# Storing transposed tokens once in fp32, with plain fp32 products for the router and the shared expert

## The reference

```python
# layernorm of x, q = x Wq, k and v from a context of 77 rows plus one null row, 16 heads of 64
x = x + jnp.tanh(g_xattn[0]) * _L0_xattn_ref(_layernorm(x, axis=-1), ctx_2048, ...)
x = x + jnp.tanh(g_ffn[0]) * _L0_ffn_ref(_layernorm(x, axis=-1), ...)

# inside _L0_ffn_ref; T = 8192 tokens, H = 256, I = 128, E = 32 experts, K = 8
logits = jnp.dot(x.astype(jnp.float32), Wr) + br
aff = jax.nn.sigmoid(logits)
top_v, top_i = jax.lax.top_k(aff, K)
top_w = top_v / (jnp.sum(top_v, axis=-1, keepdims=True) + 1e-09)
shared = jnp.dot(silu(jnp.dot(x, Wg_s) + bg_s) * (jnp.dot(x, Wu_s) + bu_s), Wd_s) + bd_s
gate = silu(jnp.einsum('th,ehi->eti', x, Wg) + bg[:, None, :])
up = jnp.einsum('th,ehi->eti', x, Wu) + bu[:, None, :]
down = jnp.einsum('eti,eih->eth', gate * up, Wd) + bd[:, None, :]
routed = jnp.einsum('te,eth->th', w_full, down)
return (shared + routed).reshape(b, s, h)
```

## Time and profile before

| | |
|---|---|
| median of 3 runs | 2115.05 us |
| the profiled execution, its own time | 2113.24 us |
| its span, first to last instruction | 2111.5 us |
| PE busy | 1992.3 us, 94% |
| DVE busy | 1669.5 us, 79% |
| ACT busy | 1387.4 us, 66% |
| POOL busy | 1205.2 us, 57% |
| DMA | 625.61 MB, 296 GB/s over the span |
| granted PE clock, mean | 0.982 |

### The profile page before, as it was taken

One profiled execution on the slowest core, in us unless ns is written; L12 is line 12 of the kernel. 1 busy time (PEld: TensorE's weight loads), 2 busy tenths in 40 slices (PEclk: granted clock), 3 DMA queues, 4 the chain that ended last, 5 costly groups with the idle time before them and its releaser, 6 DMA issues.

```text
span 2111.5 us, 42587 instructions
## 1 busy us (share of the span) xinstructions
PE 1992.3 (94%) x13762; PEld 1831.6 (87%) x13762; DVE 1669.5 (79%) x3996; ACT 1387.4 (66%) x4030; POOL 1205.2 (57%) x1323
## 2 busy tenths in 40 slices
PE   7999699999999999999996899999999999999995
PEld 7888589999999999999986789889898888888884
DVE  4333158888888888888887766668999999999996
ACT  4322277777777777777773367777777777777771
POOL 0100104777777777777777400017777777777775
PEclk9999899999999999999998999999999999999997
DMA  9664788877787777777786999999999999999998
GB/s 276 214 191 174 254 241 273 282 241 242 240 246 245 240 240 245 245 245 246 236 268 226 353 323 287 284 295 385 404 404 402 400 393 391 399 394 388 399 359 282
DMA packets 401108, 625.61 MB, mean 296 GB/s; under 512 B 170999, under 2 KB 275160, under 8 KB 398424
## 3 DMA queue, kind: packets, MB, share of 16 engines
q1 hardware_dynamic: 351736, 488.60, 68.5%
q0 software_dynamic: 49152, 134.28, 17.7%
HBM read 315.08 MB, written 307.63 MB: 295 GB/s over the span
## 4 chain that ended last, share of the span: by engine, by line
PE 42%; DVE 19%; DMA 14%; POOL 11%; issue 8%; SPq 3%; ACT 3%; DVEq 0%; POOLq 0%; ACTq 0%
DMA w_raw<-in_experts 13%; POOL pages_dram L929 6%; PE ring L147 4%; PE ring L149 3%; PE ring L148 3%; PE bank L147 3%; PE bank L149 3%; PE bank L148 3%; DVE parts L1881 3%; PE xps L1978 3%; DVE minus_max L1094 2%; PE sim L1355 2%; DVE outT_l L1241 2%; PE gate_ps L147 2%; PE yps L147 2%
## 5 line engine op out<-in xcount | busy, mean ns | idle before, releaser
L1772 POOL DMA_INDIRECT parts<-results_dram,kept_index x512 | 515.7, 1007 | 383.3 <-DMA results_dram<-y 221.9
L929 POOL DMA_INDIRECT pages_dram<-rows,kept_index x512 | 511.1, 998 | 156.0 <-issue 139.1
L1010 ACT ACTIVATE exps<-sim,minus_max 128x78 f32<-128x78 f32 x1024 | 321.7, 366 | 28.1 <-DVE minus_max L1094 27.4
L1010 ACT ACTIVATION_READ_ACCUMULATOR exps<-sim,minus_max 128x1 f32 x1024 | 252.4, 247 | 0.0
L1793 ACT ACTIVATE w_h<-w_raw 128x768 fp32r<-128x768 f32 x159 | 134.1, 843 | 146.9 <-DMA w_raw<-in_experts 146.6
L1881 DVE SCALAR_TENSOR_TENSOR parts<-parts,kept_weight 128x256 f32<-128x256 f32 x448 | 214.1, 478 | 2.1 <-DMA parts<-dense_dram 1.0
L1978 PE MATMUL xps<-ident,xin 128*128 128x128 f32 x1272 | 166.9, 274 | 17.4 <-DVE wq_l L1843 7.4
L1855 DVE TENSOR_TENSOR w_l<-w_raw,w_h 128x768 fp32r<-128x768 f32 x159 | 151.9, 956 | 37.1 <-ACT w_h L1793 36.7
L147 PE MATMUL yps<-w_h,hid_h 128*128 128x256 f32 x636 | 180.6, 284 | 0.1
L148 PE MATMUL yps<-w_h,hid_l 128*128 128x256 f32 x636 | 179.8, 283 | 0.0
L149 PE MATMUL yps<-w_l,hid_h 128*128 128x256 f32 x636 | 179.7, 283 | 0.0
(11 more groups left out here) (261 smaller groups left out, 6576.7 us busy)
## 6 DMA issues: line engine op xcount, KB each, us to landing
xin<-pages_dram SPq DMA_DIRECT2D x159, 512.0 KB, 10.8
results_dram<-y SPq DMA_DIRECT2D x159, 512.0 KB, 9.7
w_raw<-in_experts SPq DMA_DIRECT2D x159, 385.0 KB, 9.5
pages_dram<-blank SPq DMA_DIRECT2D x108, 512.0 KB, 3.3
pages_dram<-blank SPq DMA_DIRECT2D x20, 1024.0 KB, 6.5
values_dram<-values SPq DMA_DIRECT2D x16, 1024.0 KB
v_main<-values_dram SPq DMA_DIRECT2D x64, 256.0 KB
keys_dram<-keys SPq DMA_DIRECT2D x16, 616.0 KB, 4.5
```

The lines of the kernel that those rows point to most:

```text
L929: pool.indirect_dma_start(dram["pages"], bass.IndirectOffsetOnAxis(ap=kept_index[:, at:at + 1].bitcast(U32), axis=0), buffer(batch)[:, k / ...
L1010: last = act.activation(exps[u % 2][:, h, :], scores(u)[:, h // 4, h % 4, :], ACT.Exp, bias=minus_max[u][:, h:h + 1], accum_out=row_sum[u] ...
L1772: pool.indirect_dma_start(parts[slot(batch, t)][:, k, :], None, done, bass.IndirectOffsetOnAxis(ap=kept_index[:, at:at + 1].bitcast(U32), ...
```

## The change

The transposed tokens are one fp32 tile `x2T`, stored to one DRAM tensor. DVE makes no low part of them, and L multiplies `x2T` by the raw router weight in fp32: four matmuls instead of eight, one bias addition instead of two. In the dense rounds `gate_up` multiplies the raw shared weights (`shared_whole`) by the fp32 tokens: four fp32 matmuls instead of twelve fp32r ones, and SP loads one tile of tokens instead of two. Only the shared down weight is still split, so the two splitting instructions on ACT and DVE shrink from 768 to 256 columns. The page rounds stay as they are. Two waits move: SP stores `x2T` once ACT has evicted it, and the wait for the early zero fill goes from ACT to `load_ahead` on SP.

```diff
-    x2T = [sb(f"x2T_{s}", [P, DC, N], F32R) for s in "hl"]
+    x2T = sb("x2T", [P, DC, N])
-    router_w = sb("router_split", [P, DC, 2, ROUTED], F32R)
...
         def load_ahead():
+            sp.wait_ge(stores.filled_ahead, 16 * FLIGHT * AHEAD_FILLS // AHEAD_PAGES)
...
-                sp.wait_ge(ring_lo, nth(EVICTED, "N2", b))
-                for cols, part in zip(x2_cols, x2T):
-                    sp.dma_start(cols[:, :, (b - 2) * N:(b - 1) * N], part[:, :, :].bitcast(F32)).then_inc(x2_stored, 16)
+                sp.wait_ge(ring_hi, nth(EVICTED, "N2", b))
+                sp.dma_start(x2_cols[:, :, (b - 2) * N:(b - 1) * N], x2T[:, :, :]).then_inc(x2_stored, 16)
...
-            act.wait_ge(stores.filled_ahead, 16 * FLIGHT * AHEAD_FILLS // AHEAD_PAGES)
-            act.activation(ahead["shared_split"][0][:, :], shared[:, :], ACT.Copy).then_inc(shared_hi, 1)
+            act.activation(ahead["shared_split"][0][:, :], shared[:, 2 * DC * I:EW], ACT.Copy).then_inc(shared_hi, 1)
...
-                dve.tensor_tensor(logits[:, :, :], parts[:, 0], router_bias[:, :].unsqueeze(1).broadcast_to([P, TT, ROUTED]),
+                dve.tensor_tensor(logits[:, :, :], products, router_bias[:, :].unsqueeze(1).broadcast_to([P, TT, ROUTED]),
                                   ALU.add).then_inc(route_made, 1)
-                made_by("biased", b)
-                dve.tensor_tensor(logits[:, :, :], parts[:, 1], logits[:, :, :], ALU.add).then_inc(route_made, 1)
...
-            if name[0] == "Q" or not runs(name, b):
+            if name[0] == "Q" or name == "N2" or not runs(name, b):
                 return skip()
...
-            dve.tensor_tensor(ahead["shared_split"][1][:, :], shared[:, :],
+            dve.tensor_tensor(ahead["shared_split"][1][:, :], down,
...
-                pe.wait_ge(ring_lo, nth(EVICTED, "N2", b))
+                pe.wait_ge(ring_hi, nth(EVICTED, "N2", b))
                 for t in range(TT):
-                    out = ps[:, 2 * t * ROUTED:2 * (t + 1) * ROUTED]
                     for c in range(DC):
-                        pe.matmul(out, x2T[0][:, c, t * P:(t + 1) * P], router_w[:, c, :, :].rearrange("p a e -> p (a e)"),
-                                  start=c == 0, stop=False)
-                    for c in range(DC):
-                        last = pe.matmul(out[:, 0:ROUTED], x2T[1][:, c, t * P:(t + 1) * P], router_w[:, c, 0, :],
-                                         start=False, stop=c == DC - 1)
+                        last = pe.matmul(ps[:, t * ROUTED:(t + 1) * ROUTED], x2T[:, c, t * P:(t + 1) * P], router[:, c, :],
+                                         start=c == 0, stop=c == DC - 1)
...
-            for cols, part in zip(x2_cols, xT[n % XT]):
-                sp.dma_start(part[:, :, :].bitcast(F32), cols[:, :, tokens * PAGE:(tokens + 1) * PAGE]).then_inc(xT_loaded[n % XT], 16)
+            sp.dma_start(xT[n % XT][0][:, :, :].bitcast(F32), x2_cols[:, :, tokens * PAGE:(tokens + 1) * PAGE]).then_inc(xT_loaded[n % XT], 16)
...
                 for c in range(DC):
                     col = (part * DC + c) * I
+                    if is_dense(turn, s):
+                        last = pe.matmul(gu[s % 2][part][:, :], shared[:, col:col + I], xT[n % XT][0][:, c, :].bitcast(F32),
+                                         start=c == 0, stop=c == DC - 1)
+                        continue
```

More of the change, by code:

```diff
@@ L110 @@
                "PV1a": ["key"], "PV1b": ["kept"]}
-ROUTE = ["biased", "logits", "top", "without_top", "mask", "placed", "opened", "over", "page", "moved", "owner", "page_shift",
+ROUTE = ["logits", "top", "without_top", "mask", "placed", "opened", "over", "page", "moved", "owner", "page_shift",
          "over_shift", "cursor", "grown", "slot", "key", "page_end", "top_key", "kept"]
@@ L572, in attention_phase @@
     x1 = [sb(f"x1_{i}", [P, TT, D]) for i in range(2)]
-    x2T = [sb(f"x2T_{s}", [P, DC, N], F32R) for s in "hl"]
+    x2T = sb("x2T", [P, DC, N])
     router = sb("router_raw", [P, DC, ROUTED])
-    router_w = sb("router_split", [P, DC, 2, ROUTED], F32R)
     router_bias = sb("router_bias", [P, ROUTED])
-    shared = sb("shared", [P, EW])
+    shared = ahead["shared_whole"]
     bias_rows = sb("bias_rows", [3 * ROUTED, D])
@@ L652, in attention_phase @@
     x1_tiles = dram["x1"].rearrange("(b t p) d -> b p t d", t=TT, p=P)
-    x2_cols = [dram[f"x2T_{s}"].rearrange("c p n -> p c n") for s in "hl"]
+    x2_cols = dram["x2T"].rearrange("c p n -> p c n")
     weight_tiles = dram["weights"].rearrange("(b t p) e -> b p t e", t=TT, p=P)
@@ L687, in destination @@
         by_two = ps[:, :].rearrange("p (c n) -> p c n", c=2)
-        if name in ("X", "N2"):
-            return by_two, [t[:, :, :] for t in (xnT if name == "X" else x2T)]
+        if name == "X":
+            return by_two, [t[:, :, :] for t in xnT]
+        if name == "N2":
+            return by_two, [x2T[:, :, :]]
         if name in ("T1b", "T3b"):
@@ L835, in step @@
                 sp.wait_ge(ring_full, nth(RING, "Q3", B - 2))
-                sp.wait_ge(x2_stored, 32 * (B - 3))
+                sp.wait_ge(x2_stored, 16 * (B - 3))
                 for i, tile in enumerate(xT_ahead(wq)):
-                    for cols, part in zip(x2_cols, tile):
-                        sp.dma_start(part[:, :, :].bitcast(F32), cols[:, :, i * PAGE:(i + 1) * PAGE]).then_inc(x2_ahead, 16)
+                    sp.dma_start(tile[0][:, :, :].bitcast(F32), x2_cols[:, :, i * PAGE:(i + 1) * PAGE]).then_inc(x2_ahead, 16)
             if -1 <= b <= B - 3:
@@ L1378, in free @@
                     else:
-                        pe.wait_ge(ring_hi if held[0] == "Q" else ring_lo, nth(EVICTED, held, at))
+                        pe.wait_ge(ring_hi if held[0] in "QN" else ring_lo, nth(EVICTED, held, at))
                     return
@@ L1496, in sem @@
         return across.enter_context(nc.semaphore(name))
-    shared_split, bias_stack, shared_bias = ahead["shared_split"], ahead["bias_stack"], ahead["shared_bias"]
+    shared, shared_split, bias_stack, shared_bias = ahead["shared_whole"], ahead["shared_split"], ahead["bias_stack"], ahead["shared_bias"]
     xin = [sb(f"xin{i}", [P, PQ, D]) for i in range(DEPTH)]
@@ L1627, in load_x2 @@
                 sp.wait_ge(up_full, n - XT + 1)
[L1628 to L1630 removed]
+            sp.wait_ge(stores.x2, 16 * (BATCHES * (tokens + 1)))
+            sp.dma_start(xT[n % XT][0][:, :, :].bitcast(F32), x2_cols[:, :, tokens * PAGE:(tokens + 1) * PAGE]).then_inc(xT_loaded[n % XT], 16)
         def load_weights(n):
@@ L1984, in gate_up @@
                 pe.wait_ge(stores.shared_split, 1)
-                pe.wait_ge(stores.x2_ahead, 32 * early)
+                pe.wait_ge(stores.x2_ahead, 16 * early)
             if is_dense(turn, s):
                 if n >= early:
-                    pe.wait_ge(xT_loaded[n % XT], 32 * token_loads(turn, s))
+                    pe.wait_ge(xT_loaded[n % XT], 16 * token_loads(turn, s))
             else:
@@ L1993, in gate_up @@
                 pe.wait_ge(hid_lo, n - 1)
-            w = shared_split if is_dense(turn, s) else w_split[s]
             for part, done in ((0, gate_full), (1, up_full)):
@@ L2013, in down @@
                 pe.wait_ge(x_lo, DC * (m + 1))
-            w = shared_split if is_dense(turn, s) else w_split[s]
+            w = [t[:, :] for t in shared_split] if is_dense(turn, s) else [t[:, 2 * DC * I:EW] for t in w_split[s]]
             for q in range(PQ):
                 cols = slice(q * P, (q + 1) * P)
-                last = split_product(pe, yps[:, q, :], [h[:, cols] for h in hid[s % 2]], [t[:, 2 * DC * I:EW] for t in w],
+                last = split_product(pe, yps[:, q, :], [h[:, cols] for h in hid[s % 2]], w,
                                      start=True, stop=not is_dense(turn, s))
@@ L2056, in layer @@
                     *(across.enter_context(nc.semaphore(n)) for n in ("kept_weighed", "kept_summed")))
-        ahead = {"shared_split": [sb(f"shared_{s}", [P, EW], F32R) for s in "hl"],
+        ahead = {"shared_whole": sb("shared_whole", [P, EW]),
+                 "shared_split": [sb(f"shared_{s}", [P, D], F32R) for s in "hl"],
                  "shared_bias": sb("shared_bias", [P, 2]),
@@ L2080, in layer @@
                 context = context_phase(nc, ctx, across, dram, ident, wq, wo, rows, norm, opened_by, hoisted,
-                                        ahead["shared_split"][0], stores.filled_ahead)
+                                        ahead["shared_whole"], stores.filled_ahead)
             with ExitStack() as ctx:
@@ L2135 @@
     dram["keys"] = nc.dram_tensor("keys_dram", (B, P, PAIRS * M), F32, kind="Internal").ap()
-    for part in "hl":
-        dram[f"x2T_{part}"] = nc.dram_tensor(f"x2T_{part}_dram", (DC, P, T), F32, kind="Internal").ap()
+    dram["x2T"] = nc.dram_tensor("x2T_dram", (DC, P, T), F32, kind="Internal").ap()
     dram["values"] = nc.dram_tensor("values_dram", (B * M, 2 * INNER), F32, kind="Internal").ap()
```

16 lines of the change are left out of this document (7 added, 9 removed).

## The result

The changed kernel takes 2101.99 us by the median of 4 runs (2101.22 to 2105.63), beside 2116.13 for the kernel before in the same comparison: a ratio of 0.9934, 95% interval 0.9918 to 0.995. The forecast was 2107, with a range of 2101 to 2117. The medians lie 14.1 us apart and the interval of the ratio spans 10.6 to 17.4 us, so some 3 us aren't traced to any stage; the profiled execution of before is a quick one, 2.9 us under its median.

A forecast was written before the change was run, and what follows sets the result against it. PE was taken to bound attention, DMA and SP to delay the first page. From the profiled 2113.24 us, -5.4 (first page) and -3.8 (tail) gave 2104.0, 2105.9 on the median's scale, placed at 2107; range 2101 to 2117.

The forecast's parts named there:

- The price of an fp32 product: Dense rounds' gate_up: two records per fp32 product, 3.44 us against 2.80 to 2.88, so +0.6 us a round.
- L: Router product in attention: four fp32 products make eight records again, 0 taken, from a range of 0 to +6 us.
- DVE's work in attention: Attention: the 0.68 and 0.22 us taken off DVE in 32 iterations are covered by POOL's rstd and PE, 0.
- The start of the dense rounds: PE's wait of 1.28 us ahead of gate_up(0), for the split of the shared weights, goes: -1.3 us.
- Rounds 2 to 5: Dense rounds where PE waits for DVE: longer gate_up disappears in waits, DVE loses work, -0.7 us.
- Rounds 6 to 10: Dense rounds where PE sets the pace: 5 x 0.6, +3.2 us with rounding.
- The first page: Its load is issued near 1205 us, PE's 5.36 us wait goes (-3.5), full clock (-1.9): -5.4 us.
- The tail: Late tokens arrive 2 to 4 us earlier, gain capped by the last gather's landing: -3.8 us.
- only one wait goes: Rival: only the first page's wait or the tail's wait goes, 2110 or 2111 us; chance 0.17.
- PE does pay: Rival: no wait gives way, 16 dense rounds of +0.6 stand on the path, +10, so 2125 us; chance 0.09.
- L costs more: Rival: slower load of fp32 stationary operands in attention, 0.133 a record or more, +6 and up, 2112 to 2115; chance 0.08.
- fp32 products cost half: Rival: one record per fp32 product, L falls to 0.44 us, rounds 6 to 10 shorten, about 2090 us; chance 0.04.

The follow-up runs named there:

- all tokens twice: The changed kernel with each dense round's 512 KB of tokens loaded a second time and PE waiting for both loads: 2111.71 us, 0.9986 of before.

## Why the prediction was right, step by step

**The price of an fp32 product** was right: two records each, and the two products of `gate_ps` take 1.72 us (1202.91 to the first of `up_ps` at 1204.63), 0.43 us a record of 512 columns, 3.44 us for a `gate_up`. **L** was right at 0. The Trainium skill (Perfetto Trace Analysis, Engine Utilization) halves the array's output rate for FP32_LOW_HIGH, by which a `gate_up` would take 1.7 us, an estimate; the trace of this case doesn't agree, with 3.44 us.

**DVE's work in attention** was right at 0, shown by the run that put it back.

**The start of the dense rounds**, -1.3: the wait went, but `gate_up(0)` began only 1.1 us earlier, 0.3 of it in this stage. The granted clock between 1120 and 1125 us was 0.66 in this execution and 1.00 in that of before, and from N2's transposes (1119.73) to L (1127.40) it took 7.7 us instead of 6.1 (1120.97 to 1127.08). The gain was lost beside that lower clock; two executions of edited kernels whose attention is the same, with 0.88 and 1.00 there, took 893.1 and 893.3 us for this stage, 2.7 to 2.9 less than before. `gate_up(1)` took 4.8 us (3.08 to `up_ps` at 1144.37, and 1.72) where I had 5.4 and before had 4.68.

**Rounds 2 to 5**, -0.7: round 6 started 2.2 us earlier, not 1.3. The term left out is the clock again. The shorter wait of 2.87 us was followed by full clock, and `yps` at 1162.26 to `gate_ps` at 1165.51 took 3.25 us where before it was 4.52.

**Rounds 6 to 10**, +3.2: the price per round was right, but the sum came to 2.5 us (30.2 against 27.7 from `gate_up(6)`), and to the same 2.5 by the run with twelve fp32r matmuls. The term overlooked is a wait of PE in round 7, 1.18 us before and 0.53 after, in which one round's 0.6 disappears.

**The first page**, -5.4 with what stands before it: the mechanism was right and the size too small. SP issued it at 1204.06 (I had 1205), the transposes came at 1214.01 (I had 1215.6: 0.9 of the difference is the earlier round 6, 0.7 the cheaper rounds 6 to 10), and the clock gave its 1.9 us. The first gather was 7.0 us earlier and the last one 5.1, since the gathers between them took 1.9 us longer in this execution; others have 679.7 to 682.8 us.

**The tail**, -3.8: also too small, by 2.4 us. The term that failed is the last gather's landing. I took the median of 5.8 us over all gathers; the last one landed in 3.27 us, so the bound by which I cut the tail's gain lay at 2093.8 and not 5.8 us behind its issue (2096.3). The trace of before could have told: its gathers issued between 1500 and 1600 us have a median of 6.1 us to landing, those between 2085 and 2090.4 us one of 4.0.

Together the first page (7.0 instead of 5.4) and the tail (6.2 instead of 3.8) gave 4.0 us more than the sum, and the gathers between them took 1.9 back. That round 6 came so early is in part the luck of a clock that stayed full in this execution.

**The rivals.** That only one wait goes is excluded: with the late loads put back the time rises clear of noise, and with the early ones PE waits for the page again (2.45 and 3.05 us), though the time alone leaves that half open. PE does pay in rounds 6 to 10, but not everywhere. That L costs more, or that fp32 products cost half, is excluded by the records.

**What stays open.** With all tokens twice the kernel was 3 us faster than before, by a ratio whose interval ends at 0.9995. Between 1 and 5 us of the whole gain, net of what PE pays for its longer products, is thus not in the loads of tokens. The end of the wait ahead of `gate_up(0)` and DVE's shorter work in rounds 0 to 5 are the candidates; no run separated them from the clock's own variation.

## What to carry to other kernels

Where a precision split is undone, count the bytes and PE's records separately: here PE pays 0.6 us a round for fp32 products and the halved loads give back more than that, as the DMA engines were full (a share of 1.05 to 1.08) in the two stretches that hold up what follows. When a wait is bounded by a transfer, take its landing time from the same stretch, not from the median of the whole kernel. A shortened wait can be worth more than its length, where the clock behind it no longer falls (0.80 from 1160 to 1165 us before, 1.00 after); it isn't sure to, as the next section shows.

## What the runs showed of the hardware that I had not expected

The same wait of PE (2.84 to 2.87 us) was followed by half clock in two executions and by full clock in four, and the drop puts PE 4.5 us back. From `xn` to `gate_up(0)` kernels with the same attention code take 893.1 to 899.1 us, and where I looked, the granted clock in the last two iterations went with it (1120 to 1125 us: 0.50 in the two longest, 0.88 and 1.00 in the two shortest). Among the others the order is less clear (0.66 at 895.6 and 896.3 us, 0.80 at 896.8). The two longest are also the two kernels that issue two more loads of tokens in that stretch, near 1088 us; the kernel before issues them too and had 896.0 us with a clock of 1.00, so the loads alone don't settle it. Events of two executions are thus compared by their distance from a near event, not by their absolute times.

After the change, from 1180 to 1200 us, SP's issues take 0.6 to 2.9 us each while the DMA engines are at a share of 0.99 to 1.08 (2.86 us for one load of weights at 1185.23; 1.37, 1.03 and 1.28 for the loads of tokens). The next load of tokens, at 1200.78, takes 0.36 us. The DMA engines are as full there (1.08 from 1200 to 1201 us), but SP had issued nothing for 1.15 us. So a slow issuer here looks like a symptom of what is already queued on the DMA engines; no run tests that by itself. Splitting a load in two issues left the first page's time as it was.
